# Weighing in an attention kernel: both halves' high weights first, the wait for the low weights behind them

## The chip, the cores and the metric

The kernel runs on one core of a Trainium2 chip. Its five engines run side by side and meet at semaphores: TensorE (PE: matmuls; its weight loads are shown as PEld), VectorE (DVE), ScalarE (ACT), GpSimd (POOL) and SyncE (SP, which issues the DMAs). The metric is the device time of one execution in microseconds (us), as the median of several runs.

## The reference

```
x = x + attention(group_norm(x))                     # x: (4, 256, 64, 64), 32 groups
def attention(x):                                    # xf: x as (4, 256, 4096), called tokens below
    f = einsum('qc,bcn->bqn', Wq, xf)                # 64 channels
    g = einsum('qc,bcn->bqn', Wk, xf)                # 64 channels
    h = einsum('vc,bcn->bvn', Wv, xf)                # 256 channels
    beta = softmax(einsum('bqn,bqm->bnm', f, g), axis=1)      # over n
    return gamma * einsum('bvn,bnm->bvm', h, beta) + xf
```

For every column m of each of the four images, 4096 scores over n are exponentiated, normalised and used as weights of the 4096 values h.

## The kernel before

**Tiling.** The kernel takes 256 columns m at a time. Such a block is called a column here and numbered k, 0 to 63, 16 to an image. The 4096 rows n of a column are cut into 8 groups g of 512 rows; a group of a column is a *slot* n = 8k + g, of which there are 512. All of a slot's tiles are 128 x 1024: four tiles of 128 rows, each with 256 columns.

**The path of a slot.** PE makes the scores of two slots at once into the two halves of S (`scores`, lines 474 to 480, 16 matmuls), at the head of every even slot and 16 to 17 slots ahead of their use. ACT copies them out to SC (`store`, line 614) and DVE keeps a running maximum (`maximum`, lines 778 and 783). When all 8 groups of a column are there, DVE turns the maxima (`turn_maxima`), reduces them (`quadrant_maxima`), PE shares them among the partitions with two small matmuls (`share_maxima`, line 501), and DVE reduces and spreads the result (`column_maxima`, `spread_maxima`). Then, four slots ahead of the weighing, DVE subtracts the maximum (`subtract`, line 823), and three slots ahead ACT takes the exponential twice (`exps`): rounded to 16 bits as the high weights PH (line 620), and in full in place (line 621). POOL subtracts the one from the other, which gives the low weights PL (`low_weights`, line 377). PH and PL have room for four slots; the exponentials of slot n + 3 wait until slot n - 1 has been weighed (semaphore `weighed`).

**The weighing.** A slot is weighed in two halves m = 0, 1 of 128 columns, each into a bank of O of its own. A half takes its four tiles in turn, and for each tile three matmuls: high weights by high values (line 492), high weights by low values (493), low weights by high values (494). That is 12 matmuls to a half and 24 to a slot. Ahead of a slot PE waits for `pl_ready`, which implies the high weights too.

**What stands between.** PE's order is written out by hand in its loop over the slots. Between the halves (MID) and behind them (END) stand at fixed places the projections of the next image (`extra`: lines 436 to 441 and 451 to 453; a projection of values waits until the one before has been drained by ACT at line 631 and DVE at line 834, semaphore `v_done`). In slot g = 3 of each column the sharing of the maxima of column k + 1 stands between the halves. It waits for the last of that column's eight groups to be stored and maximised: those scores were made at the head of slot g = 2. Each of the engines runs its own list strictly in the order in which it is written.

**The first slot.** Slot 0 is cut into FIRST and REST, two tiles each: DVE subtracts (line 928), ACT exponentiates (667 to 671) and POOL makes low weights (405, 407) for one part after the other, and PE starts on the first part when its low weights are there (`pl_first`). It also waits until the bank of each half has been cleared of a projection: `v_done` 14 for the first half, 15 for the second and for the rest of the slot. The last projection of values, the sixteenth, lies in the third bank; DVE drains it behind `subtract(2)` and two maxima.

Of the kernel before, what the change touches and what calls it, by code (L numbers as in the profile page):

```python
# [5 lines left out]
def groupnorm_attention(nc, x, wqT, wkT, wvT, gamma, out):  # L6
    f32, f16, i32 = mybir.dt.float32, mybir.dt.float16, mybir.dt.int32
    ALU, ACT, AX = mybir.AluOpType, mybir.ActivationFunctionType, mybir.AxisListType

    BATCH, C, N = x.shape  # L10
    P = 128
    H = C // P
    CQ = wqT.shape[1]
    M = 256
    CPB = N // M
    K = BATCH * CPB
    T = N // P
    GT = 4
    G = T // GT
    GW = GT * M  # L20
# [52 lines left out]
    with ExitStack() as ctx:  # L73
# [121 lines left out]
        def sc(s):  # L195

            k, g = divmod(s, G)
            first = (k % 2) * T * M + g * GW
            return SC[:, first:first + GW]
# [14 lines left out]
        def first_v(u):  # L214
            return first_bank(2 * u + 2) if u < VU else O[:, (u + 2) % OB, :]

        FIRST = slice(0, GW // 2)
        REST = slice(GW // 2, GW)

        def halves(u):  # L220

            top, bottom = slice(0, CQ), slice(CQ, P)
# [2 lines left out]
        def bank(k, m):  # L225

            return O[:, (MB2 * k + m) % OB, :]
# [120 lines left out]
        @block.gpsimd  # L348
        def _(pool):
            pool.memset(V[:, :].rearrange("p (t w) -> p t w", w=VW)[:, :, C:C + 1], 1.0).then_inc(consts, 1)  # L350
            pool.memset(ident[:, :], 0.0).then_inc(consts, 1)
            pool.wait_ge(consts, 2)
            pool.affine_select(out=ident[:, :], in_=ident[:, :], compare_op=ALU.not_equal, fill=1.0,
                               base=0, pattern=[[-1, P]], channel_multiplier=1).then_inc(consts, 1)
            pool.memset(alike[:, :], 0.0).then_inc(consts, 1)
            for i, shift in enumerate(range(QP - P, P, QP)):
                pool.wait_ge(consts, 4 + i)
                pool.affine_select(out=alike[:, :], in_=alike[:, :], compare_op=ALU.not_equal, fill=1.0,
                                   base=shift, pattern=[[-1, P]], channel_multiplier=1).then_inc(consts, 1)

            pool.wait_ge(w_hi, 1)
            pool.tensor_tensor(wqkl[:, :, :], wqk[:, :, :], wqkh[:, :, :], ALU.subtract).then_inc(w_split, 1)
            pool.tensor_tensor(wvl[:, :, :], wv[:, :, :], wvh[:, :, :], ALU.subtract).then_inc(w_split, 1)
            pool.wait_ge(res_coefs, 1)
            for u in range(NFG):
                if u >= 2:
                    pool.wait_ge(xl_ready[1], u - 1)
                pool.tensor_scalar(x1n[:, u % 2, :], x0[:, 1, unit(u)], nrstd[:, 1:2], rbias[:, 0, 1:2],
                                   ALU.mult, ALU.add).then_inc(x1n_ready, 1)
                pool.wait_ge(x1n_ready, u + 1)  # L370
                pool.wait_ge(xh_ready, H * u + 2)
                pool.tensor_tensor(XL[:, 1, unit(u)], x1n[:, u % 2, :], XH[:, 1, unit(u)],
                                   ALU.subtract).then_inc(xl_ready[1], 1)

            def low_weights(s):
                pool.wait_ge(exp_done, s + 1)
                pool.tensor_tensor(PL[:, s % RING, :], sc(s), PH[:, s % RING, :], ALU.subtract).then_inc(pl_ready, 1)  # L377

            def residual(k):
                b = k // CPB  # L380
                pool.wait_ge(res_coefs, b + 1)
                pool.wait_ge(xres_in, 16 * (k + 1))
                if k >= 2:
                    pool.wait_ge(out_stored[k % 2], 16 * (k // 2))
                for h in range(H):
                    r = pool.tensor_scalar(RES[:, k % 2, h, :], xres[:, h, :], rscale[:, b % 2, h:h + 1],
                                           rbias[:, b % 2, h:h + 1], ALU.mult, ALU.add)
                r.then_inc(res_ready, 1)

            def add_attention(k):  # L390
                for q in range(NQ):
                    pool.wait_ge(att_in[q], 16 * NQ * (k + 1))
                pool.wait_ge(res_ready, k + 1)
                flat = "p h m q n -> p (h m q n)"
                r = RES[:, k % 2, :, :].rearrange("p h n -> p (h n)")
                pool.tensor_tensor(r, r, ATT[:, :, :, :, :].rearrange(flat), ALU.add).then_inc(out_ready, 1)  # L396

            def low_input(b, p):
                for h in range(H):
                    pool.wait_ge(xh_ready, H * NFG + H * (NPC * (b - 1) + p) + h + 1)  # L400
                    pool.tensor_tensor(XL[:, h, piece(p)], xin[:, h, :], XH[:, h, piece(p)],
                                       ALU.subtract).then_inc(xl_ready[h], 2)

            pool.wait_ge(exp_first, 1)
            pool.tensor_tensor(PL[:, 0, FIRST], sc(0)[:, FIRST], PH[:, 0, FIRST], ALU.subtract).then_inc(pl_first, 1)
            pool.wait_ge(exp_done, 1)
            pool.tensor_tensor(PL[:, 0, REST], sc(0)[:, REST], PH[:, 0, REST], ALU.subtract).then_inc(pl_ready, 1)
            for s in range(1, EXP_LEAD):
                low_weights(s)
            for n in range(K * G):  # L410
                k, g = divmod(n, G)
                b, j = divmod(k, CPB)
                if n + EXP_LEAD < K * G:
                    low_weights(n + EXP_LEAD)
                if g == 4:
                    residual(k)
                if g == 5 and k > 0:
                    add_attention(k - 1)
                if g == 6 and b + 1 < BATCH and NORM_FIRST <= j < NORM_FIRST + NPC:
                    low_input(b + 1, j - NORM_FIRST)  # L420

        @block.tensor
        def _(pe):
# [56 lines left out]
                        m = mm(to(a, i), F1[:, rows(a, i)], G1[:, cols], start=False, stop=True)  # L480
                    m.then_inc(s_ready, 1)

            def weigh(n, m, tiles=range(GT)):

                k, g = divmod(n, G)
                o = bank(k, m)
                for i in tiles:
                    t = g * GT + i
                    vh = V[:, t * VW:t * VW + C + 1]
                    vl = V[:, t * VW + VL0:t * VW + VL0 + C]  # L490
                    cols = slice(i * M + m * P, i * M + (m + 1) * P)
                    mm(o[:, 0:C + 1], PH[:, n % RING, cols], vh, start=t == 0, stop=False)  # L492
                    mm(o[:, 0:C], PH[:, n % RING, cols], vl, start=False, stop=False)  # L493
                    w = mm(o[:, 0:C + 1], PL[:, n % RING, cols], vh, start=False, stop=t == T - 1)  # L494
                if m == MB2 - 1 and GT - 1 in tiles:
                    w.then_inc(weighed, 1)

            def share_maxima(c, o):
# [61 lines left out]
            for n in range(K * G):  # L560
# [5 lines left out]
                if q is not None:  # L566
# [4 lines left out]
                    if q % G == 0 and i % 2 == 0:  # L571
                        pe.wait_ge(g_in[i // 2], 16 * (nb + 1))
                    scores(q)
                if n == 0:
                    pe.wait_ge(pl_first, 1)
                    for m in range(MB2):
                        pe.wait_ge(v_done, NV - 2 + m)
                        weigh(0, m, range(GT // 2))
                pe.wait_ge(pl_ready, n + 1)
                if g == 0:  # L580
                    if j == FG_FIRST + 1 and b + 1 < BATCH:
                        pe.wait_ge(fg_done, (b + 1) * NFG + 7)
                    if j == FG_FIRST + 2 and b + 1 < BATCH:
                        pe.wait_ge(fg_done, (b + 2) * NFG)
                if j == 0:
                    pe.wait_ge(v_done, b * NV + max(2 * g + 2, len(V_AT)) if b else NV - 1 if n == 0 else NV)
                if g == 0 and j == 1:
                    pe.wait_ge(v_done, (b + 1) * NV)
                tiles = range(GT) if n > 0 else range(GT // 2, GT)
                weigh(n, 0, tiles)  # L590
                extra(k, g, MID)
                if n == 4:
                    share_maxima(1, shared0)
# [4 lines left out]
                    share_maxima(k + 1, S[:, 0, :])  # L598
                if g == 0 and k > 0:
                    pe.wait_ge(osb_ready, MB2 * (k - 1) + 1)  # L600
                weigh(n, 1, tiles)
                extra(k, g, END)
            turn_output(K - 1)

# [1 line left out]
        def _(act):  # L606
# [56 lines left out]
            store(G)  # L663
            round_v(NV - 1, first_v(NV - 1))
            store(G + 1)
            act.wait_ge(sub_first, 1)
            nc.scalar.activation(PH[:, 0, FIRST], sc(0)[:, FIRST], ACT.Exp, bias=SHIFT)
            nc.scalar.activation(sc(0)[:, FIRST], sc(0)[:, FIRST], ACT.Exp, bias=SHIFT).then_inc(exp_first, 1)
            act.wait_ge(sub_ready, 1)
            nc.scalar.activation(PH[:, 0, REST], sc(0)[:, REST], ACT.Exp, bias=SHIFT)  # L670
            nc.scalar.activation(sc(0)[:, REST], sc(0)[:, REST], ACT.Exp, bias=SHIFT).then_inc(exp_done, 1)
            exps(1)
            store(G + 2)
            store(G + 3)
# [22 lines left out]
        def _(dve):  # L697
# [223 lines left out]
            maximum(G + 1)  # L921
            column_maxima(0, shared0)
            spread_maxima(0)
            dve.wait_ge(mb_ready, 1)
            dve.wait_ge(s_stored, 1)
            for part, done in ((FIRST, sub_first), (REST, sub_ready)):
                half = sc(0)[:, part].rearrange("p (i m) -> p i m", i=GT // 2)
                ve.tensor_tensor(half, half, MB[:, 0:M].unsqueeze(1).to_broadcast([P, GT // 2, M]),
                                 ALU.subtract).then_inc(done, 1)
            subtract(1)  # L930
            low_v(NV - 3, first_v(NV - 3))
            low_v(NV - 2, first_v(NV - 2))
# [91 lines left out]
```

## Time and profile before

| | us |
|---|---|
| median of 3 runs | 1938.38 |
| lowest and highest | 1937.92, 1938.48 |
| the profiled execution's own time | 1938.83 |
| its span in the trace | 1937.0 |

| engine | busy us | share |
|---|---|---|
| PE | 1890.4 | 98% |
| DVE | 1589.5 | 82% |
| ACT | 1571.4 | 81% |
| POOL | 1305.3 | 67% |

The profiler follows one execution. A span of busy time is the union of an engine's instructions; a matmul's own duration (0.27 us) is longer than the distance between two starts (0.11 us), since they are pipelined, so PE can lose some tenths of a microsecond between two matmuls with no idle time on record. Distances between starts show such losses, and times of busy engines don't. Times in the rows are from the start of the span.

### The profile page before, as it was taken

Reading aid. Unit: us, or ns where it says so; the run is one execution under the profiler, and the core shown is the slowest. Engines: PE = TensorE matmul, PEld = TensorE weight load, DVE = VectorE, ACT = ScalarE, POOL = GpSimd, SP = SyncE. Lnnn points to the kernel's source line nnn. Section 1 sums busy time; section 2 is a strip of 40 time slices with the busy share of each in tenths; the row PEclk is TensorE's granted clock in tenths of the full one; section 3 lists DMA queues with packets and bytes.
Section 4 is the critical chain, followed back from the end, with each engine's and each line's share of the span. In section 5 each row is a group of like instructions: output and inputs, shape, how many; then the busy total and the mean of one; then the engine's idle time right before and its main releaser. Section 6 shows DMA issues by size and latency. Waiting matters only on the chain. (4 is left out here: it accounts for less than half of the span.)

```text
span 1937.0 us, 44170 instructions
## 1 busy us (share of the span) xinstructions
PE 1890.4 (98%) x17476; PEld 1562.9 (81%) x17476; DVE 1589.5 (82%) x1932; ACT 1571.4 (81%) x1677; POOL 1305.3 (67%) x761
## 2 busy tenths in 40 slices
PE   5999999999999999999999999999999999999998
PEld 3678888878878888887887888888788888888887
DVE  7888998877768899987876889998777787888784
ACT  4788889977768888897876888898787788888885
POOL 4367668866646677886654776788565577766777
PEclk9999999999999999999999999999999999999999
DMA  4022112212111211211211211121130011111111
GB/s 143 4 67 77 45 33 74 55 23 67 29 46 49 74 53 29 72 53 31 60 35 39 78 45 54 53 55 45 28 78 18 21 31 33 31 26 31 32 34 34
DMA packets 199021, 91.18 MB, mean 47 GB/s; under 512 B 150176, under 2 KB 191392, under 8 KB 198816
## 3 DMA queue, kind: packets, MB, share of 16 engines
q1 hardware_dynamic: 198816, 88.36, 17.4%
q8 instruction: 139, 2.28, 0.5%
q14 instruction: 66, 0.54, 0.1%
HBM read 46.60 MB, written 16.78 MB: 33 GB/s over the span
## 5 line engine op out<-in xcount | busy, mean ns | idle before, releaser
L377 POOL TENSOR_TENSOR PL<-SC,PH 128x1024 f16<-128x1024 f32 x511 | 1088.8, 2137 | 572.2 <-ACT SC L621 568.1
L492 PE MATMUL O<-V,PH 128*128 128x257 f16 x4096 | 1119.1, 273 | 4.3 <-DVE OSB L856 3.1
L494 PE MATMUL O<-V,PL 128*128 128x257 f16 x4096 | 1119.0, 273 | 0.0
L493 PE MATMUL O<-V,PH 128*128 128x256 f16 x4096 | 1117.2, 273 | 0.0
L620 ACT ACTIVATE PH<-SC 128x1024 f16<-128x1024 f32 x511 | 539.1, 1055 | 123.1 <-PE O L494 116.8
L823 DVE TENSOR_TENSOR SC<-SC,MB 128x1024 f32<-128x1024 f32 x511 | 613.6, 1211 | 0.1
L614 ACT ACTIVATE SC<-S 128x1024 f32<-128x1024 f32 x512 | 502.0, 1012 | 115.4 <-issue 102.0
L783 DVE TENSOR_TENSOR XM<-S,XM 128x1024 f32<-128x1024 f32 x384 | 468.4, 1220 | 127.4 <-PE S L480 126.1
L621 ACT ACTIVATE SC<-SC 128x1024 f32<-128x1024 f32 x511 | 533.0, 1043 | 0.0
L492 PEld LDWEIGHTS O<-V,PH 128*128 128x128 f16 x4096 | 406.3, 99 | 53.9 <-DVE OSB L856 4.4
L493 PEld LDWEIGHTS O<-V,PH 128*128 128x128 f16 x4096 | 401.1, 98 | 50.2
L494 PEld LDWEIGHTS O<-V,PL 128*128 128x128 f16 x4096 | 401.0, 98 | 50.1
L474 PE MATMUL S<-GG,F 128*128 128x256 f16 x1024 | 154.3, 273 | 6.1 <-ACT SC L614 2.5
L480 PE MATMUL S<-GG,F 128*128 128x256 f16 x1024 | 156.4, 275 | 0.0
L477 PE MATMUL S<-GG,F 64*128 64x256 f16 x2048 | 156.3, 272 | 0.0
L778 DVE TENSOR_TENSOR XM<-S,SC 128x1024 f32<-128x1024 f32 x64 | 78.4, 1224 | 87.3 <-ACT SC L614 87.2
L480 PEld LDWEIGHTS S<-GG,F 128*128 128x128 f16 x1024 | 79.2, 98 | 59.9 <-issue 54.0
L477 PEld LDWEIGHTS S<-GG,F 64*128 64x128 f16 x2048 | 79.1, 94 | 59.8 <-issue 53.9
L474 PEld LDWEIGHTS S<-GG,F 128*128 128x128 f16 x1024 | 98.9, 98 | 24.1 <-issue 6.5
L834 DVE TENSOR_TENSOR V<-O,V 128x512 f16<-128x512 f32 x62 | 42.4, 689 | 59.3 <-ACT V L631 59.0
L631 ACT CAST V<-O 128x512 f16<-128x512 f32 x62 | 35.9, 586 | 61.9 <-PE O L453 61.6
L396 POOL TENSOR_TENSOR RES<-RES,ATT 128x512 f32<-128x512 f32 x63 | 80.5, 1278 | 0.4 <-DMA ATT<-OT 0.4
(106 smaller groups left out, 1100.8 us busy)
## 6 DMA issues: line engine op xcount, KB each, us to landing
xin<-x SPq DMA_DIRECT2D x24, 1024.0 KB, 5.6
xres<-x SPq DMA_DIRECT2D x64, 256.0 KB, 2.8
out<-RES SPq DMA_DIRECT2D x64, 256.0 KB, 2.2
ATT<-OT SPq DMA_DIRECT2D x1008, 16.0 KB, 1.9
F<-GG SPq DMA_DIRECT2D x64, 64.0 KB, 2.0
GG<-GG SPq DMA_DIRECT2D x32, 128.0 KB, 2.4
SC<-x SPq DMA_DIRECT2D x3, 1024.0 KB, 7.3
SC<-x SPq DMA_DIRECT2D x2, 512.0 KB, 10.5
```

The source lines that it names most:

```text
L377: pool.tensor_tensor(PL[:, s % RING, :], sc(s), PH[:, s % RING, :], ALU.subtract).then_inc(pl_ready, 1)
L474: mm(to(a, i), F1[:, rows(a, i)], G1[:, cols], start=True, stop=False)
L477: mm(to(a, i), F1[half, rows(a, i)], GL[half, cols], start=i % 2 == 1, stop=i % 2 == 0)
L480: m = mm(to(a, i), F1[:, rows(a, i)], G1[:, cols], start=False, stop=True)
L492: mm(o[:, 0:C + 1], PH[:, n % RING, cols], vh, start=t == 0, stop=False)
L493: mm(o[:, 0:C], PH[:, n % RING, cols], vl, start=False, stop=False)
L494: w = mm(o[:, 0:C + 1], PL[:, n % RING, cols], vh, start=False, stop=t == T - 1)
L614: nc.scalar.activation(sc(q), S[:, q % 2, :], ACT.Copy).then_inc(s_stored, 1)
L620: nc.scalar.activation(PH[:, s % RING, :], sc(s), ACT.Exp, bias=SHIFT)
L621: nc.scalar.activation(sc(s), sc(s), ACT.Exp, bias=SHIFT).then_inc(exp_done, 1)
L783: ve.tensor_tensor(XM[:, :], scores, XM[:, :], ALU.max).then_inc(s_maxed, 1)
L823: ve.tensor_tensor(tile, tile, MB[:, 0:M].unsqueeze(1).to_broadcast([P, GT, M]), ALU.subtract).then_inc(sub_ready, 1)
```

## The change

A slot's 24 matmuls are the same ones, in another order. `weigh` is split into `weigh_high` (8 matmuls of a half, both products of the high weights) and `weigh_low` (4 matmuls of a half). In slots g > 0 the order is high of half 0, high of half 1, low of half 0, low of half 1; in slots g = 0 it is high and low of half 0, then high and low of half 1. The wait ahead of the slot is now for `exp_done`, the high weights, and the wait for `pl_ready` stands ahead of the first low matmul: behind 16 matmuls, or behind 8 where g = 0. What stood between the halves stands behind the 8 high matmuls of half 0 where g > 0. The first slot is no longer cut in two: it takes the way of the others on every engine, and PE waits ahead of it for `v_done` 16.

```diff
-            def weigh(n, m, tiles=range(GT)):
+            def weigh_high(n, m):
...
                     mm(o[:, 0:C + 1], PH[:, n % RING, cols], vh, start=t == 0, stop=False)
                     mm(o[:, 0:C], PH[:, n % RING, cols], vl, start=False, stop=False)
-                    w = mm(o[:, 0:C + 1], PL[:, n % RING, cols], vh, start=False, stop=t == T - 1)
-                if m == MB2 - 1 and GT - 1 in tiles:
+
+            def weigh_low(n, m):
...
+                    w = mm(o[:, 0:C + 1], PL[:, n % RING, cols], V[:, t * VW:t * VW + C + 1], start=False,
+                           stop=t == T - 1)
+                if m == MB2 - 1:
                     w.then_inc(weighed, 1)
...
-                if n == 0:
-                    pe.wait_ge(pl_first, 1)
-                    for m in range(MB2):
-                        pe.wait_ge(v_done, NV - 2 + m)
-                        weigh(0, m, range(GT // 2))
-                pe.wait_ge(pl_ready, n + 1)
+                pe.wait_ge(exp_done, n + 1)
...
                 if j == 0:
-                    pe.wait_ge(v_done, b * NV + max(2 * g + 2, len(V_AT)) if b else NV - 1 if n == 0 else NV)
+                    pe.wait_ge(v_done, b * NV + max(2 * g + 2, len(V_AT)) if b else NV)
...
-                tiles = range(GT) if n > 0 else range(GT // 2, GT)
-                weigh(n, 0, tiles)
+                weigh_high(n, 0)
+                if g == 0:
+                    pe.wait_ge(pl_ready, n + 1)
+                    weigh_low(n, 0)
                 extra(k, g, MID)
...
-                weigh(n, 1, tiles)
+                weigh_high(n, 1)
+                if g > 0:
+                    pe.wait_ge(pl_ready, n + 1)
+                    weigh_low(n, 0)
+                weigh_low(n, 1)
                 extra(k, g, END)
```

On ACT, DVE and POOL the parts FIRST and REST of slot 0 go, and `exps(0)`, `subtract(0)` and `low_weights(0)` take their place.

**First place: PE in slot g = 3 of a column, before and after the sharing of the maxima.** PH and PL are the high and low weights, V the values, `alike` and `mxs` what the sharing multiplies. Before:

```order
L492 MATMUL O<-V,PH 128x257 [waits pl_ready]
L493 MATMUL O<-V,PH 128x256
L494 MATMUL O<-V,PL 128x257
...
L501 MATMUL S<-mxs,alike 128x32 [waits mxs_ready,s_maxed,s_stored]
L492 MATMUL O<-V,PH 128x257
L493 MATMUL O<-V,PH 128x256
L494 MATMUL O<-V,PL 128x257
...
L474 MATMUL S<-GG,F 128x256 [waits s_stored,s_maxed,mxc_ready]
```

and now, where line 485 is what was 492, 486 what was 493, 495 what was 494, 503 what was 501 and 467 what was 474:

```order
L485 MATMUL O<-V,PH 128x257 [waits exp_done]
L486 MATMUL O<-V,PH 128x256
...
L503 MATMUL S<-mxs,alike 128x32 [waits mxs_ready,s_maxed,s_stored]
L485 MATMUL O<-V,PH 128x257
L486 MATMUL O<-V,PH 128x256
...
L495 MATMUL O<-V,PL 128x257 [waits pl_ready]
L495 MATMUL O<-V,PL 128x257 x7
L467 MATMUL S<-GG,F 128x256 [waits s_stored,s_maxed,mxc_ready]
```

The sharing has moved from behind the twelfth matmul of the slot to behind the eighth, and 16 matmuls stand between it and the next scores in place of 12.

**Second place: PE at the start of slot 0.** Before:

```order
L480 MATMUL S<-GG,F 128x256 x4
L492 MATMUL O<-V,PH 128x257 [waits v_done,pl_first]
L493 MATMUL O<-V,PH 128x256
L494 MATMUL O<-V,PL 128x257
...
L492 MATMUL O<-V,PH 128x257 [waits v_done]
...
L492 MATMUL O<-V,PH 128x257 [waits v_done,pl_ready]
```

and now:

```order
L473 MATMUL S<-GG,F 128x256 x4
L485 MATMUL O<-V,PH 128x257 [waits v_done,exp_done]
L486 MATMUL O<-V,PH 128x256
...
L495 MATMUL O<-V,PL 128x257 [waits pl_ready]
L495 MATMUL O<-V,PL 128x257 x3
```

Three waits for `v_done` (14, 15 and 15) have become one for 16 ahead of everything, and the wait for low weights has gone behind 8 matmuls.

**Third place: DVE at the same point.** Line 834 (832 now) drains projections of values: numbers 14 and 15 in the row that ends in x2, number 16 in the last row; line 783 (781) is the maximum. Before:

```order
L928 TENSOR_TENSOR SC<-SC,MB 128x512 [waits s_stored,mb_ready]
L928 TENSOR_TENSOR SC<-SC,MB 128x512
L823 TENSOR_TENSOR SC<-SC,MB 128x1024 [waits s_stored,mb_ready]
L834 TENSOR_TENSOR V<-O,V 128x2x256 [waits v_hi] x2
L783 TENSOR_TENSOR XM<-S,XM 128x1024 [waits s_maxed,s_ready]
L823 TENSOR_TENSOR SC<-SC,MB 128x1024 [waits s_stored,mb_ready]
L783 TENSOR_TENSOR XM<-S,XM 128x1024 [waits s_maxed,s_stored,s_ready]
L834 TENSOR_TENSOR V<-O,V 128x2x256 [waits v_hi]
```

and now:

```order
L821 TENSOR_TENSOR SC<-SC,MB 128x1024 [waits s_stored,mb_ready] x2
L832 TENSOR_TENSOR V<-O,V 128x2x256 [waits v_hi] x2
L781 TENSOR_TENSOR XM<-S,XM 128x1024 [waits s_maxed,s_ready]
L821 TENSOR_TENSOR SC<-SC,MB 128x1024 [waits s_stored,mb_ready]
L781 TENSOR_TENSOR XM<-S,XM 128x1024 [waits s_maxed,s_stored,s_ready]
L832 TENSOR_TENSOR V<-O,V 128x2x256 [waits v_hi]
```

The two half subtractions are one whole one; the sixteenth drain still stands behind both maxima.

## Rows read from the trace of the kernel before

**Rows 1.** The page: busy time and share of an engine, and one group of instructions.
```profile
PE 1890.4 (98%) x17476; PEld 1562.9 (81%) x17476; DVE 1589.5 (82%) x1932; ACT 1571.4 (81%) x1677; POOL 1305.3 (67%) x761
...
L494 PE MATMUL O<-V,PL 128*128 128x257 f16 x4096 | 1119.0, 273 | 0.0
```

**Rows 2.** PE's waits: line, releaser, us in total, times, longest.
```profile
PE O L451 <- DVE V L834: 5.0, 15, 0.9
...
PE O L492 <- POOL PL L405: 1.1, 1, 1.1
```

**Rows 3.** Timeline of a usual column: start, us, engine, line, [idle before <-releaser].
```profile
190.65 1.06 ACT L620 ACTIVATE PH<-SC 128x1024 f16<-128x1024 f32 x1 [0.63 <-PE O L494]
...
192.56 1.00 ACT L614 ACTIVATE SC<-S 128x1024 f32<-128x1024 f32 x1
193.76 1.23 DVE L778 TENSOR_TENSOR XM<-S,SC 128x1024 f32<-128x1024 f32 x1 [1.52 <-ACT SC L614]
194.90 2.34 DVE L823 TENSOR_TENSOR SC<-SC,MB 128x1024 f32<-128x1024 f32 x2
...
199.12 1.22 DVE L783 TENSOR_TENSOR XM<-S,XM 128x1024 f32<-128x1024 f32 x1
...
201.38 1.22 DVE L783 TENSOR_TENSOR XM<-S,XM 128x1024 f32<-128x1024 f32 x1
...
202.54 0.27 PE L494 MATMUL O<-V,PL 128*128 128x257 f16 x1
...
202.70 0.38 PE L501 MATMUL S<-mxs,alike 128*128 128x32 f32 x2
```

**Rows 4.** Timeline: the first and the last sharing of this kind.
```profile
120.42 0.38 PE L501 MATMUL S<-mxs,alike 128*128 128x32 f32 x2 [1.05 <-ACT SC L614]
...
1873.05 0.27 PE L494 MATMUL O<-V,PL 128*128 128x257 f16 x1
...
1873.38 0.27 PE L494 MATMUL O<-V,PL 128*128 128x257 f16 x1
1873.54 0.38 PE L501 MATMUL S<-mxs,alike 128*128 128x32 f32 x2
```

**Rows 5.** Timeline: the last maximum and a sharing that does not wait.
```profile
257.22 1.22 DVE L783 TENSOR_TENSOR XM<-S,XM 128x1024 f32<-128x1024 f32 x1
...
258.70 0.31 PE L501 MATMUL S<-mxs,alike 128*128 128x32 f32 x2
```

**Rows 6.** Timeline around the start of slot 0.
```profile
68.25 1.28 DVE L928 TENSOR_TENSOR SC<-SC,MB 128x512 f32<-128x512 f32 x2
68.97 0.63 ACT L667 ACTIVATE PH<-SC 128x512 f16<-128x512 f32 x1 [0.23 <-DVE SC L928]
69.73 0.61 PE L480 MATMUL S<-GG,F 128*128 128x256 f16 x4
71.41 0.28 PE L492 MATMUL O<-V,PH 128*128 128x257 f16 x1 [1.06 <-POOL PL L405]
72.96 1.91 ACT L614 ACTIVATE SC<-S 128x1024 f32<-128x1024 f32 x2
74.05 1.23 DVE L783 TENSOR_TENSOR XM<-S,XM 128x1024 f32<-128x1024 f32 x1
75.19 0.68 DVE L834 TENSOR_TENSOR V<-O,V 128x512 f16<-128x512 f32 x1
75.72 0.60 PE L474 MATMUL S<-GG,F 128*128 128x256 f16 x4
```

**Rows 7.** Stretches: length, busy us (and count) by engine, PE's granted clock, DMA share, GB/s.
```profile
71.40:75.10 3.70, 3.69 (x19) 2.65 (x20) 3.70 (x4) 3.70 (x5) 3.04 (x2) 0.54 0.02 4
...
246.00:250.00 4.00, 2.97 (x31) 2.24 (x26) 3.79 (x11) 2.69 (x3) 3.67 (x2) 1.00 0.01 2
```

**Rows 8.** Timeline: 12 matmuls of slot 3 of a new image, and the projection behind them.
```profile
561.33 0.27 PE L492 MATMUL O<-V,PH 128*128 128x257 f16 x1
...
562.94 0.27 PE L451 MATMUL O<-wvh,XH 128*128 128x256 f16 x1
```

More of the change, by code:

```diff
@@ L215, in first_v @@
             return first_bank(2 * u + 2) if u < VU else O[:, (u + 2) % OB, :]
-        FIRST = slice(0, GW // 2)
-        REST = slice(GW // 2, GW)
         def halves(u):
@@ L402, in low_input @@
                                        ALU.subtract).then_inc(xl_ready[h], 2)
[L404 to L408, printed above, removed]
+            for s in range(EXP_LEAD):
                 low_weights(s)
@@ L481, in scores @@
                     m.then_inc(s_ready, 1)
-            def weigh(n, m, tiles=range(GT)):
+            def weigh_high(n, m):
                 k, g = divmod(n, G)
                 o = bank(k, m)
-                for i in tiles:
+                for i in range(GT):
                     t = g * GT + i
@@ L493, in weigh @@
                     mm(o[:, 0:C], PH[:, n % RING, cols], vl, start=False, stop=False)
-                    w = mm(o[:, 0:C + 1], PL[:, n % RING, cols], vh, start=False, stop=t == T - 1)
-                if m == MB2 - 1 and GT - 1 in tiles:
+            def weigh_low(n, m):
+                k, g = divmod(n, G)
+                o = bank(k, m)
+                for i in range(GT):
+                    t = g * GT + i
+                    cols = slice(i * M + m * P, i * M + (m + 1) * P)
+                    w = mm(o[:, 0:C + 1], PL[:, n % RING, cols], V[:, t * VW:t * VW + C + 1], start=False,
+                           stop=t == T - 1)
+                if m == MB2 - 1:
                     w.then_inc(weighed, 1)
@@ L665, in _ @@
             store(G + 1)
[L666 to L671, printed above, removed]
+            exps(0)
             exps(1)
@@ L923, in _ @@
             spread_maxima(0)
[L924 to L929, printed above, removed]
+            subtract(0)
             subtract(1)
```

## The prediction

> **What bounds the kernel now.** I read the page first: PE is busy for 98% of the span and no other engine for more than 82% [rows 1]. So what is asked of every other engine is only whether PE comes to wait for it, and of PE what it does beside its matmuls. Second the waits of PE: in all the execution it waits for POOL's low weights once, for 1.1 us [rows 2]. That once is the start of slot 0 [rows 6]. A wait that goes behind two thirds of a slot therefore has 1.1 us to win, and not some tenths in each of 512 slots. Third the timeline of PE for the distance between starts, since a wait below some 0.15 us leaves no bracket: three weighing matmuls take 0.33 us from start to start, 0.11 each [rows 4]. Where a matmul starts later than that behind its forerunner, PE has waited.
>
> **The sharing of the maxima (the main term).** The change moves it from behind the twelfth matmul of slot g = 3 to behind the eighth, 4 x 0.11 = 0.44 us earlier for PE. Is it ready earlier? In the usual column the last maximum starts at 201.38 and takes 1.22, so it ends at 202.60, and the sharing starts at 202.70 [rows 3]. The matmul before it started at 202.54, so that it could have started at 202.65: PE already waits there for DVE, by 0.05 us. Of the 62 sharings into S between 120.42 and 1898, 49 stand like this, 0.10 us behind the end of the maximum; the first and the last of these are shown [rows 4].
>
> What sets the end of that maximum? Followed back, DVE has no idle time from 193.76 on: the first maximum of the slots to come, two subtractions, the turning of the output, a reduction, and then maximum, subtraction, maximum [rows 3]. It began at 193.76 since it had waited 1.52 us for ACT's store of 192.56, which stood behind two exponentials, and these had waited for the end of the previous column's weighing: ACT idle 0.63 us on line 494 [rows 3]. `weighed` is still raised by the last matmul of a slot. So the chain from the end of a column to its sharing is 190.65 to 202.70 of ACT and DVE work with nothing of PE's in it that the change moves, and PE arrives 0.44 us too early at its end. The wait grows by 0.44 us in each of the 49 columns. What stands behind it is all of PE's list, and the next chain starts at the end of this column, later by as much; nothing gives it back. 49 x 0.44 = **21.6 us**.
>
> Three columns have the sharing with slack: the maximum ends at 257.22 + 1.22 = 258.44, so PE could start at 258.54 and does at 258.70 [rows 5]. There 0.44 - 0.16 = 0.28, three times **0.8 us**. The other ten come over 1.5 us behind the maximum and stay free.
>
> **The start.** Three edits meet here. (a) DVE subtracts slot 0 whole; two whole tiles take 2.34 [rows 3], so one ends some 1.2 us behind 68.25, at 69.46, where the half allowed ACT to start at 68.97 [rows 6]. (b) ACT's two whole exponentials take 192.56 - 190.65 = 1.91 from start to start [rows 3]; from 69.54 they end at 71.45. (c) PE then waits for `v_done` 16, and not for POOL. Exponentials alone would let it start near 71.6, 0.2 behind the 71.41 of before [rows 6]. But the sixteenth drain stands on DVE behind both maxima at 75.19 and takes 0.68 [rows 6], and the second maximum needs ACT's first store. That store came at 72.96 behind exponentials of slot 1 that started 1.9 before, at 71.06; now they start at 71.45, so the store at 73.35, its end 74.36, the second maximum 74.45 in place of 74.05, the drain 1.14 behind it, 75.59 to 76.27, and PE at about 76.35. Start of slot 0: **4.94 us later**.
>
> Now the clock. PE has nothing to do from 70.3 to 71.4, and had waited twice before; from 71.65 its clock is at 1.2 GHz until 75.05 (granted 0.54 over 71.40 to 75.10 [rows 7]). Slot 0 took 75.72 - 71.41 = 4.31 us where 24 x 0.11 = 2.64 would do [rows 6]: 1.67 lost. Now PE is idle for 6.1 us. I take it that the low level lasts as long behind the start as before, 3.4 us, costing 1.7: the term stays 4.94 + 1.7 - 1.67 = **5.0 us**. Bounds: no low level, 3.3; the whole slot at it, 24 x 0.22 = 5.3, gives 5.9. Nothing later gives this back: up to the first sharing DVE's and ACT's gaps end on PE's scores, so that they move with PE.
>
> **Projections of values in a new image.** `v_done` is what their PE waits are for: 15 times, 5.0 us in all [rows 2]. In slots 1, 3 and 5 one stands at MID and one at END. At MID 8 matmuls stand ahead of it and not 12, so PE waits longer and the projection starts at the same time. Then 16 stand between it and END. In slot 3, 12 matmuls from 561.33 end at 562.65 and the projection starts at 562.94; 16 end at 563.09 [rows 8]: 0.15 late. Slot 5 is alike, in slot 1 the wait is longer than 0.44 us and takes it. 3 images x 2 x 0.15 = **0.9 us**. Bounds: nothing, and all 15 waits longer by 0.44, 6.6.
>
> **At nothing:** the second semaphore wait of a slot (512 of them): a matmul behind a wait that is met starts 0.11 behind its forerunner like any other. Low weights: POOL has them three slots ahead, and now may be 1.8 us later. The other place at which PE waited for them by some 0.3 us is column 0, and there the next scores wait for ACT's store, whose time is DVE's, so nothing comes of it. In slots g = 0 the wait for the output of the last column stays behind 12 matmuls. Matmul count and shapes are the same.
>
> **Sum.** 21.6 + 0.8 + 5.0 + 0.9 = 28.3 us on the profiled execution's own 1938.83: 1967.1. That execution lies 0.45 above the median of 1938.38, so 1966.7 as a median.
>
> **Rivals.** (1) *The sharing costs nothing*: DVE's chain shortens by what PE comes earlier. For it speaks only that DVE has idle time elsewhere; against it that the chain is closed from 193.76 on [rows 3]. Then 1938.4 + 5.0 + 0.9 = 1944.3. Chance 0.08. (2) *The start costs nothing* since the drain isn't what holds PE: 1966.7 - 5.0 = 1961.7; against it stands the order on DVE. 0.06. (3) *Projections pay every time*: 1966.7 + 5.7 = 1972.4; 0.06. (4) *Not slower*: the matmuls lie closer. Runs of 8 high and 4 low matmuls take the place of the pattern high, high, low. The place is all 12288 weighing matmuls, the price 12.3 us for each nanosecond of distance, and the point from which it decides 28.3 us / 12288 = 2.3 ns. 257 columns at 2.4 GHz are 107.1 ns and three matmuls took 0.33 us [rows 4], so at the very best 29 us come back and the time is some 1937. Against it: each of the three kinds follows its forerunner at the same distance today, whatever weights came before. 0.02. (5) *The clock falls at each sharing*. At the start idle time was followed by 1.2 GHz and a loss of 1.67 us; 49 such losses are 82 us, 2048. Against it: over 246 to 250 PE was busy for only 2.97 of 4.00 us, with a granted clock of 1.00 [rows 7], and the new wait is a third of that gap. 0.02. The Trainium skill (TensorE: Matmul & The Clock Gate, A second HAM failure mode: psum-queue depth-cycling) tells of a kernel whose frequent short idles between groups of matmuls made the clock swing between its two levels; here the trace disagrees so far, since a gap of 1.0 us left it at the high level.
>
> **How the numbers follow.** The forecast, 1966.7, has 0.76. The range takes in the bounds: below, a start of 3.3 and sharings that cost 0.39 (0.44 less the 0.05 already lost), 49 x 0.39 = 19.1: 1938.4 + 22.4 = 1961; above, the start at 5.9 and rival 3: 1973. Rivals 2 and 3 lie in it, 0.88 in all. A measurement of this kernel tells 0.2%, 4 us, from no change; faster by more has 0.02, within it 0.02, slower by more 0.96 (rival 1 is slower too, by 0.3%).
>
> **What would show it.** In the trace of the changed kernel PE's sharing should start still 0.10 us behind the end of the last maximum, but some 0.5 us behind the matmul before it plus 0.11, in about 49 columns, each longer by 0.44 us. PE's waits should list the sharing with some 20 us and low weights with nothing. Slot 0's first matmul should start at about 76.35, right behind the sixteenth drain, with the clock low behind it. If the last maximum ends earlier relative to the end of the previous column, the main step is wrong; if slot 0 starts near 71.6, the start is.

## The result: slower by 1.4%, as forecast

The changed kernel takes 1964.47 us in the median of four runs (1964.14 to 1965.87) against 1938.38 us before: 1.0136 times, 95% interval 1.0121 to 1.0151, or 26.1 us more. The forecast was 1966.7, the range 1961 to 1973. The profiled execution took 1964.14 us with a span of 1962.4, 25.4 above the span of before.

The page of the changed kernel, its part on busy time, answers to [rows 1]:

```profile
PE 1896.5 (97%) x17476; PEld 1563.7 (80%) x17476; DVE 1589.3 (81%) x1931; ACT 1572.1 (80%) x1675; POOL 1306.0 (67%) x760
```

The same 17476 matmuls run in a span longer by 25 us, and no other engine does more. So the time went into waits of PE. Its waits in the changed kernel (line, releaser: us in total, times, longest us) answer to [rows 2]:

```profile
PE S L503 <- issue: 16.4, 48, 0.6
PE O L444 <- DVE V L832: 7.1, 12, 0.7
PE O L485 <- DVE V L832: 5.0, 1, 5.0
...
PE O L485 <- DVE OSB L854: 1.8, 3, 0.6
...
PE S L503 <- ACT SC L617: 1.5, 1, 1.5
```

And the waits of the kernel before that these stand against:

```profile
PE O L492 <- DVE OSB L856: 3.1, 3, 1.0
...
PE S L474 <- issue: 1.2, 2, 1.0
```

The sharing of the maxima (line 503, 501 before) is new at the head of the list: 48 waits of 0.34 us each on record, besides what the matmul ahead covers by its own duration. "issue" means that the view names no releaser, so the releaser has to be read from the timeline. Low weights don't occur. The drain of the sixteenth projection (line 832) holds PE once, for 5.0 us: the start of slot 0.

The timeline of a usual column of the changed kernel (start, us, engine and line, idle before) answers to [rows 3]:

```profile
197.23 1.06 ACT L623 ACTIVATE PH<-SC 128x1024 f16<-128x1024 f32 x1 [0.63 <-PE O L495]
...
199.14 1.01 ACT L617 ACTIVATE SC<-S 128x1024 f32<-128x1024 f32 x1
...
200.35 1.22 DVE L776 TENSOR_TENSOR XM<-S,SC 128x1024 f32<-128x1024 f32 x1 [1.53 <-ACT SC L617]
...
207.97 1.22 DVE L781 TENSOR_TENSOR XM<-S,XM 128x1024 f32<-128x1024 f32 x1
...
208.69 0.27 PE L486 MATMUL O<-V,PH 128*128 128x256 f16 x1
209.28 0.38 PE L503 MATMUL S<-mxs,alike 128*128 128x32 f32 x2 [0.32 <-issue]
```

From ACT's exponential behind the end of the last column to the sharing it is 12.05 us here, and it was 202.70 - 190.65 = 12.05 before [rows 3]. The last maximum ends at 209.19 and the sharing starts 0.09 behind it, as it did. But the matmul ahead of it started at 208.69, 0.59 earlier, and not 0.16. The chain on ACT and DVE has not moved by a hundredth; PE comes to its end 0.44 us sooner and waits that much longer.

The start of slot 0 in the changed kernel answers to [rows 6], first the timeline, then the busy time by stretch (length, PE, PEld, DVE, ACT, POOL, granted clock of PE, DMA):

```profile
75.04 1.23 DVE L781 TENSOR_TENSOR XM<-S,XM 128x1024 f32<-128x1024 f32 x1 [0.34 <-ACT SC L617]
76.18 0.68 DVE L832 TENSOR_TENSOR V<-O,V 128x512 f16<-128x512 f32 x1
...
77.01 0.38 PE L485 MATMUL O<-V,PH 128*128 128x257 f16 x1 [4.97 <-DVE V L832]
...
80.99 0.60 PE L467 MATMUL S<-GG,F 128*128 128x256 f16 x4
```

```profile
70.40:77.00 6.60, 1.64 (x12) 0.60 (x7) 6.26 (x8) 6.60 (x8) 4.22 (x2) 0.50 0.00 0
77.00:79.60 2.60, 2.59 (x13) 1.84 (x14) 0.99 (x1) 0.76 (x1) 1.77 (x1) 0.50 0.00 0
79.60:81.00 1.40, 1.40 (x14) 1.20 (x13) 0.00 (x0) 0.00 (x0) 0.36 (x1) 0.93 0.04 12
```

PE starts slot 0 at 77.01, right behind the drain, and is at the scores of slot 1 at 80.99, where it was at 75.72 before.

### The profile page after: what moved, and what is told of

Read it like the earlier page. It is cut to its first block and busy times, and to the rows that moved or that the text cites. A ratio compares the mean times of both kernels' runs of the same rounds, so it can differ in the third digit from the quotient of the medians.

```text
span 1962.4 us, 44165 instructions
## 1 busy us (share of the span) xinstructions
PE 1896.5 (97%) x17476; PEld 1563.7 (80%) x17476; DVE 1589.3 (81%) x1931; ACT 1572.1 (80%) x1675; POOL 1306.0 (67%) x760
## 5 line engine op out<-in xcount | busy, mean ns | idle before, releaser
L485 PE MATMUL O<-V,PH 128*128 128x257 f16 x4096 | 933.4, 273 | 6.7 <-DVE V L832 5.0
L486 PE MATMUL O<-V,PH 128*128 128x256 f16 x4096 | 932.9, 273 | 0.0
L495 PE MATMUL O<-V,PL 128*128 128x257 f16 x4096 | 544.9, 273 | 0.0
```

The costliest lines, as they stand in the source:

```text
L495: w = mm(o[:, 0:C + 1], PL[:, n % RING, cols], V[:, t * VW:t * VW + C + 1], start=False, stop=t == T - 1)
```

## Experiments

All ratios are against runs of the kernel before on the same chip, whose median was 1938.8 us. The changed kernel was not run again beside them, so differences from its 1964.47 us are good to some tenths. Experiment 6 ran on another chip than the rest; the kernel before took 1938.8 us there too.

**1. The sharing behind 12 matmuls again.** The changed kernel, with slots g = 3 in the order of slots g = 0:

```diff
                 weigh_high(n, 0)
-                if g == 0:
+                if g in (0, 3):
                     pe.wait_ge(pl_ready, n + 1)
                     weigh_low(n, 0)
...
                 weigh_high(n, 1)
-                if g > 0:
+                if g not in (0, 3):
```

> The changed kernel with one thing undone: in slots g = 3 the low weights of half 0 follow its high ones, as in slots g = 0, so that the sharing of the maxima stands behind 12 matmuls again and not behind 8. Theory (the sharing waits for the last maximum, whose time PE's order does not move): the wait of 0.44 us goes in 49 columns, less 0.3 for three columns that gave some back, and 0.45 of the projections of values in slot 3 goes too: 1964.5 - 21.2 - 0.45, about 1942.8. Rival (the order of the products, high high and low apart, makes the matmuls or their waits dearer): 504 of 512 slots and more keep it, so nearly nothing goes, 1962 or more.

Measured: 1943.72 us, 1.0026 (1.0016 to 1.0037). 20.8 us of 26.1 went with one slot in eight put back. The expectation was 1942.8. PE's waits in this kernel have the place of the sharing almost without a wait, and the wait for the output of a column at 3.1 us, as before the change:

```profile
PE O L485 <- DVE OSB L854: 3.1, 3, 1.0
...
PE S L503 <- issue: 0.5, 3, 0.2
```

**2. The start.** The changed kernel, with the drains awaited as before:

```diff
-                    pe.wait_ge(v_done, b * NV + max(2 * g + 2, len(V_AT)) if b else NV)
+                    pe.wait_ge(v_done, b * NV + max(2 * g + 2, len(V_AT)) if b else NV - 2 if n == 0 else NV)
...
+                if n == 0:
+                    pe.wait_ge(v_done, NV - 1)
                 weigh_high(n, 1)
```

> The changed kernel with the waits of slot 0 for drained banks as before the change: 14 drains ahead of half 0, 15 ahead of half 1, in place of 16 ahead of everything; slot 0 stays uncut on all engines. Theory (the sixteenth drain held the start): slot 0 starts when its exponentials are there, some 4.8 us earlier, near 72.2 in the trace or 71.6 where the start is not late; the low clock costs it 1.7 and not 1.3 us; 1964.5 - 4.5, about 1960.0. Rival (cutting slot 0 in two was what mattered, and the uncut exponentials hold the start): at most 1 us is won, 1963.5 or more.

Measured: 1959.5 us, 1.0106 (1.0091 to 1.0122): 5.0 us of the 26.1. Slot 0 starts at 71.46, when its exponentials are there, 0.05 behind the start of before, or 0.15 when both are counted from the first sharing (66.32 here, 66.42 before); the timeline of PE shows both of its waits in the slot:

```profile
71.46 0.40 PE L485 MATMUL O<-V,PH 128*128 128x257 f16 x1 [1.21 <-ACT SC L626]
...
73.68 0.61 PE L495 MATMUL O<-V,PL 128*128 128x257 f16 x2 [0.32 <-POOL PL L374]
```

So an uncut slot 0 with its low weights behind 8 matmuls starts within 0.2 us of the cut one, and the wait for all sixteen drains was the loss.

**3. Both.** The edits of 1 and 2 together.

> The changed kernel with both undone, the sharing behind 12 matmuls and 14 and 15 drains ahead of slot 0. What is left of the change is the order of the products in all 512 slots, the wait for low weights behind two thirds, and the uncut slot 0. Theory: these are worth nothing, but for 0.2 us of a later start and 0.3 us of projections in slot 5: 1938.4 to 1939.2. Rival (the order of products costs by itself): clearly more, 1942 or above. Rival (the later wait for low weights wins): below 1937.5.

Measured: 1938.94 us, 1.0001 (0.9992 to 1.0011). The new order of the products in all slots, the wait for low weights behind two thirds of the slot and the uncut start are worth nothing either way that the interval of 2 us could show. The traces are finer. From the start of one column to that of the next, this one and that of before agree within 0.01 us in 56 of the columns 1 to 63. The three columns in which an image begins are 0.1 us longer, as expected, and the others that differ are the ones treated below under "What was not in the sum". PE waited for low weights once, 1.2 us, as often and about as long as before:

```profile
72.23 0.28 PE L485 MATMUL O<-V,PH 128*128 128x257 f16 x1 [1.21 <-ACT SC L626]
74.44 0.61 PE L495 MATMUL O<-V,PL 128*128 128x257 f16 x4 [1.16 <-POOL PL L374]
```

**4. The sharing alone.** The kernel before, its order of products untouched, with the sharing behind 9 matmuls:

```diff
-                weigh(n, 0, tiles)
+                if shares:
+                    weigh(n, 0, range(3))
+                    share_next()
+                    weigh(n, 0, range(3, GT))
+                else:
+                    weigh(n, 0, tiles)
```

> The kernel before with one part of the change alone: the sharing of the maxima moved from behind 12 matmuls of slot g = 3 to behind 9 (a tile's three stay together), nothing else. Theory: 3 x 0.11 = 0.33 us in each of 49 columns, 16.2 us, less 0.3 that the three columns give back: about 1954.3. Rival (the wait at the sharing is made good later in the column, or it is the order of the products that costs): 1938.4 to 1940.

Measured: 1953.29 us, 1.0076 (1.0061 to 1.0091), 14.5 us more, 1.4 less than the 15.9 expected; 1.2 of that was given back at two waits ahead of the scores, which are treated below. Three matmuls' worth of place costs 0.33 us a column, with everything else as it was:

```profile
203.56 0.27 PE L494 MATMUL O<-V,PL 128*128 128x257 f16 x1
204.05 0.38 PE L501 MATMUL S<-mxs,alike 128*128 128x32 f32 x2 [0.21 <-issue]
```

0.49 us from the matmul ahead, against 0.16 before.

**5. The sharing at the head of the slot.** The changed kernel, with `share_next()` ahead of `weigh_high(n, 0)`.

> The changed kernel with its suspected cost increased: the sharing at the head of slot g = 3, behind none of its matmuls in place of 8. Theory: one to one, 8 x 0.11 = 0.88 us more in each of 49 columns, 43 us, and hardly anything in the three columns whose later wait for the output shrinks by nearly as much: about 2008. Rival (PE's wait lets DVE run ahead, so that a part is given back in each column): clearly less than 2000.

Measured: 2018.03 us, 1.0409 (1.0390 to 1.0428), 53.6 us above the changed kernel, and more than the 43 of one to one. Nothing was given back in the usual column; something was added. The three columns with slack, which were expected to pay hardly anything, paid 0.84 us each by the distance of their starts, 2.5 in all. The rest lies in the usual column itself. DVE and PE there:

```profile
211.00 1.22 DVE L785 TENSOR_TENSOR XM<-S,XM 128x1024 f32<-128x1024 f32 x1
...
212.47 0.38 PE L503 MATMUL S<-mxs,alike 128*128 128x32 f32 x2 [1.35 <-DVE XM L785]
```

The sharing starts 0.25 us behind the end of the maximum and not 0.10. The matmul now waited for four semaphores.

**6. The same, with three semaphores.** The wait for `exp_done` goes behind the sharing:

```diff
-                pe.wait_ge(exp_done, n + 1)
...
+                if shares:
+                    share_next()
+                pe.wait_ge(exp_done, n + 1)
```

> As the version with the sharing at the head of slot g = 3, but PE waits for the slot's high weights behind the sharing and not ahead of it, so that the sharing's matmul waits for three semaphores and not for four. With four it started 0.26 us behind the end of the last maximum, where the sharing behind 8 or 12 matmuls starts 0.10 behind it. If the fourth semaphore is what costs, it starts 0.10 behind again and the time falls by 49 x 0.16, 7.8 us, to about 2010. If it is that PE has stood idle for over a microsecond, it stays at 0.26 and 2018.

Measured: 2010.23 us, 1.0368 (1.0338 to 1.0398), 7.8 us less. The timeline:

```profile
212.99 1.22 DVE L785 TENSOR_TENSOR XM<-S,XM 128x1024 f32<-128x1024 f32 x1
...
214.31 0.38 PE L503 MATMUL S<-mxs,alike 128*128 128x32 f32 x2 [1.20 <-ACT SC L621]
```

The sharing starts 0.10 behind the maximum again, though PE had been idle for as long. It was the fourth wait. Most columns are shorter by 0.15 or 0.16 us in this trace than in that of experiment 5; that the times themselves differ by just the 7.8 us expected is in part luck, since each is the median of two runs and those of experiment 6 lie 2.3 us apart. Whether the number of semaphores costs, or this one in this place, the two runs don't separate. The releaser that the row names is not the one that came last: the maximum is.

**7. The sharing later than before.** The kernel before, with the sharing behind 15 matmuls:

```diff
-                weigh(n, 1, tiles)
+                if shares:
+                    weigh(n, 1, range(1))
+                    share_next()
+                    weigh(n, 1, range(1, GT))
+                else:
+                    weigh(n, 1, tiles)
```

> The kernel before with the sharing of the maxima later, behind 15 matmuls of slot g = 3 in place of 12, nothing else. Theory: the last maximum is then ready 0.28 us before PE comes, so the wait of 0.05 us and the 0.07 us that a sharing behind a wait takes longer both go in 49 columns, 5.9 us, and the reduction behind the sharing still starts when DVE's subtraction ends: about 1933. Rival (what is won at the sharing is lost at the scores of the next slot, which wait for that reduction): 1938 or above.

Measured: 1934.14 us, 0.9977 (0.9968 to 0.9986). This is faster than both kernels, by 4.6 us than the one before; the expectation was 1933. A usual column:

```profile
201.69 1.22 DVE L790 TENSOR_TENSOR XM<-S,XM 128x1024 f32<-128x1024 f32 x1
...
203.18 0.27 PE L494 MATMUL O<-V,PL 128*128 128x257 f16 x1
203.29 0.31 PE L501 MATMUL S<-mxs,alike 128*128 128x32 f32 x2
```

The maximum ends 0.38 us ahead, the sharing follows at the ordinary 0.11, and its pair of matmuls takes 0.31 and not 0.38. Some 1.3 us of the 5.9 are missing; the waits for the output and for drained values have grown, from 3.1 to 3.5 and from 5.0 to 6.4 us:

```profile
PE O L451 <- DVE V L841: 6.4, 18, 0.9
PE O L492 <- DVE OSB L863: 3.5, 3, 1.2
```

**8. The changed order with the sharing late.** As 2, with the sharing between `weigh_high(n, 1)` and the low weights, behind 16 matmuls.

> The changed kernel with its order of products, the sharing moved from behind 8 to behind 16 matmuls (both halves' high weights) of slot g = 3, and the waits of slot 0 for 14 and 15 drains. Theory: like the kernel before with the sharing behind 15, plus the 0.2 us of a later start and 0.3 to 0.8 us at projections of values: about 1933.5 to 1934. Rival (the product order does cost something that the sharing hid): 1936 or above.

Measured: 1936.85 us, 0.9990 (0.9981 to 0.9999). The expectation was missed by 3 us, and the time lies where its rival was to lie, at 1936 or above: 2.7 us are between this and version 7. PE's waits for drained values have grown by 2.4, 8.8 us in place of 6.4:

```profile
PE O L444 <- DVE V L838: 8.8, 15, 0.7
```

By the distance of the starts each of the three columns in which an image begins is 0.65 us longer than in experiment 7, 2.0 in all; nearly all the other columns, which have the changed order too, are as long within 0.01 us. So it is not the order of the products that costs. The time is lost at the projections of values. In slot 3 the one at MID, behind 8 matmuls and not 12, waits 0.78 us in place of 0.34, and the one at END 0.73 in place of 0.62, where the changed kernel has none; in slot 5 the two together wait 0.10 longer.

**9. The sharing at the end of the slot.** As 7, behind all 24 matmuls.

> The kernel before with the sharing behind all 24 matmuls of slot g = 3, right ahead of the next scores. Theory: the scores then wait for the reduction of what is shared, which starts 0.34 us behind the start of the sharing, takes 0.19 and is known 0.1 later, 0.63 in place of 0.14 us: 0.5 us in each of 49 columns, 24 us above the version with the sharing behind 15: about 1957. So the place of the sharing has a window, late enough for the maximum and early enough for the reduction. Rival (later is never worse): as with 15, about 1933.

Measured: 1958.21 us, 1.0100 (1.0082 to 1.0119).

```profile
204.53 0.31 PE L501 MATMUL S<-mxs,alike 128*128 128x32 f32 x2
205.12 0.61 PE L474 MATMUL S<-GG,F 128*128 128x256 f16 x4 [0.28 <-DVE mxc L815]
```

```profile
204.88 0.19 DVE L815 TENSOR_REDUCE mxc<-S 128x8 f32<-128x32 f32 x1 [0.59 <-PE S L501]
```

The scores start 0.59 us behind the sharing, since the reduction is between them. So the place has a window: too early, PE waits for the maximum; too late, it waits for the reduction. The kernel before stood at its early edge, by 0.05 us on the wrong side.

## Why the prediction was right, and which terms were off

**The sharing in 49 columns: right.** The distance from the matmul ahead grew from 0.16 to 0.59 or 0.60 us. 49 x 0.44 = 21.4 against a forecast of 21.6. That it is the place of the sharing and not the order of the products is shown by experiments 1, 3 and 4 together: undone, the loss goes; done alone, a proportional loss comes; with the rest of the change left in and the drains awaited as before, the time is that of before.

**The three columns with slack: the step "nothing gives it back" failed there.** Their sharing did wait 0.28 us longer. But ahead of it, in slot g = 0 of the same column, PE had been waiting 1.2 us for DVE to take the output of the column before (1.0 on record). DVE was late there because its list in the column before also holds the statistics of the next image (lines 712 to 736 in the kernel before). It has no pause from ahead of that column's sharing on (from 221.18 in the trace of before, with the sharing at 230.12), so a later sharing does not move it. PE now comes 0.44 us later to that wait:

```profile
256.29 0.28 PE L485 MATMUL O<-V,PH 128*128 128x257 f16 x1 [0.59 <-DVE OSB L854]
```

It takes 1.8 us in three times and not 3.1 on record, 0.44 less each time by the distance of the starts. So 0.8 us forecast became -0.3 (0.28 of waiting and 0.07 of a longer sharing, less 0.44, three times). Experiments 1 and 7 show the reverse: the wait is at 3.1 and 3.5 us there.

**The start: right; the clock's part of it differs by execution.** The drain ended at 76.86 and slot 0 began at 77.01, where 76.35 was forecast; but this execution was 0.64 us late already at the first sharing, ahead of anything that the change touches, so the forecast is met within 0.02. The first sharing in the trace of before and in that of the changed kernel:

```profile
66.42 0.33 PE L501 MATMUL MB<-mxs,alike 128*128 128x32 f32 x2
```

```profile
67.06 0.33 PE L503 MATMUL MB<-mxs,alike 128*128 128x32 f32 x2
```

From there to slot 0 it is 4.99 us before, and 9.94 or 9.95 in all four traces of kernels that wait for the sixteenth drain (the changed one, experiments 1, 5 and 6): 4.96 later, against 4.94 forecast. The clock's part is another matter. In the changed kernel's trace the clock was at its low level from before 70.40 until some 79.8, 2.8 us into slot 0 in place of the 3.4 that I took, and slot 0 lost 80.99 - 77.01 - 2.64 = 1.34 us to it and not 1.7. In the traces of experiments 1 and 6 it was low for the whole slot, which took 5.10 us and lost 2.46; from experiment 1:

```profile
76.60:81.60 5.00, 5.00 (x24) 3.53 (x25) 0.95 (x1) 0.72 (x1) 2.12 (x1) 0.50 0.01 3
```

So the start costs 4.6 us in one execution and some 6 in another. The forecast of 5.0 lies between, near what the medians show: experiment 2 took 5.0 us off, and between experiments 1 and 3 lie 4.8. The forecast took the clock's part from one trace, and that it came so near is partly luck: it could have been off by 0.4 or by 1 us.

**Values of a new image: right.** In slot 3 the second projection starts 1.76 us, 16 matmuls, behind the first matmul that follows the sharing, with no wait:

```profile
571.45 0.27 PE L485 MATMUL O<-V,PH 128*128 128x257 f16 x1
...
573.21 0.27 PE L444 MATMUL O<-wvh,XH 128*128 128x256 f16 x1
```

Before, it was 1.61 [rows 8]: 0.15, as forecast; slot 5 cost 0.10, so 0.75 and not 0.9 in all. The waits moved from END to MID: 12 for 7.1 us in place of 15 for 5.0.

**What was not in the sum.** The trace of before holds waits for which it names no releaser, and the changed kernel's trace is 1.9 us shorter by waits that are in none of the terms above. By the distance of the starts it stands in four columns.

Two of them are waits ahead of the first scores of an image, 0.31 us in column 14 and 1.17 in column 46. What they wait for can be read from SyncE and its DMAs. SyncE issues the 16 DMAs of `regroup` (line 277) and then the two that bring `F` for those scores; the second took 2.0 us from issue to landing, and the scores start some 0.1 us behind that. In column 46 of the kernel before:

```profile
1432.47 11.48 SPq L277 DMA_DIRECT2D ATT<-OT  x16
...
1444.64 0.60 SPq L291 DMA_DIRECT2D F<-GG  x1
```

```profile
1446.77 0.38 PE L474 MATMUL S<-GG,F 128*128 128x256 f16 x2 [1.01 <-issue]
```

The DMAs of `regroup` start with the column, ahead of its sharing, so the sharing's 0.44 us do not move them, and PE comes later to the wait. The step "nothing gives it back" failed here as well: the 0.31 us of column 14 went whole, and 0.44 in column 46. Another 0.6 went there because the 16 DMAs took SyncE 10.88 us in the changed kernel's execution in place of 11.48, and the traces show no link of that with the change.

The other two are columns 18 and 58. There ACT's exponential behind the end of the column before stood 0.91 us idle in the kernel before and 0.63 in the changed one, as in the usual column; first before, then changed:

```profile
610.39 1.06 ACT L620 ACTIVATE PH<-SC 128x1024 f16<-128x1024 f32 x1 [0.91 <-PE O L494]
```

```profile
620.93 1.06 ACT L623 ACTIVATE PH<-SC 128x1024 f16<-128x1024 f32 x1 [0.63 <-PE O L495]
```

This starts the chain to the sharing, so 0.28 us a time, 0.56 in all, is saved. The 0.91 is there in all four traces of kernels built on the one before (with experiments 4, 7 and 9), and the 0.63 in all seven built on the changed one, so it comes with the change. Its cause is open.

Together, for the two traces: 21.4 - 0.3 + 4.6 + 0.75 = 26.5 for the terms that were forecast at 28.3, less 0.75 given back in columns 14 and 46, less 0.6 and 0.56, and 0.64 more for the late first sharing: 25.2 of 25.4. None of the last four was in the forecast. The late first sharing and the 0.6 belong to these two executions and not to the change, and it is luck that they cancel.

**Rivals.** The sharing costs nothing (1): false by experiment 1. The start costs nothing (2): false by experiment 2. All projections pay (3): false, since the columns in which an image begins are 0.25 us longer and not 2.2. Matmuls closer (4): three still take 0.33 us, and experiment 3 finds no gain. The clock falls at each sharing (5): it fell at none. PE's granted clock is 0.997 over the whole changed kernel and 1.00 from 120 to 1890 us:

```profile
120.00:1890.00 1770.00, 1743.22 (x16166) 1444.49 (x16163) 1454.84 (x1736) 1449.64 (x1535) 1208.99 (x684) 1.00 0.18 45
```

**What the change was about** never came into it. Low weights held PE once in the kernel before, for 1.1 us, and in experiment 3 once, for 1.2.

## What to carry to other kernels

When work of an engine that is the bound is reordered, look first at the small things that stand between its pieces and are waited for, or wait, on a chain of other engines: their place counts in matmuls, and each place lost is paid once a round. A wait too short for a bracket in the timeline (0.05 us here, 49 times) tells that the point stands exactly at the edge; move it later and look what is the next to wait for it. A wait for a whole count where a part of it would do ("all sixteen drains") puts everything that stands ahead of the last one into the path.

## What the runs showed of the hardware

A matmul that waited for three semaphores started 0.10 us behind the end of the operation that released it, one with a fourth semaphore, long met, 0.25 us behind, though PE was idle for over a microsecond in both: 7.8 us between the two kernels (experiments 5 and 6). Why the fourth is dearer, and whether another fourth would be, was not tried.

A pair of small fp32 matmuls behind a wait took 0.38 us from start to end, and 0.31 when it followed the matmuls ahead without one; the next matmul came 0.21 and 0.14 us behind its start.

The clock at the start is not the same from one execution to the next. In the profiled execution of experiment 3 it stayed at 2.4 GHz around slot 0, though PE had waited three times in the 5 us ahead of it; in those of the changed kernel and of experiments 1, 2 and 6 it was at 1.2 GHz when the slot started, with the same or longer waits ahead. Experiment 3's busy time and granted clock (1.00):

```profile
72.20:77.00 4.80, 3.61 (x30) 2.60 (x32) 4.46 (x6) 4.80 (x6) 4.23 (x2) 1.00 0.01 3
```

The Trainium skill (TensorE: Matmul & The Clock Gate, The HAM clock gate) says that the default state is throttled and that activity releases it; the stretch from 77.00 on agrees, with 0.50 at first and 0.93 from 79.60 to 81.00.
